# A two-layer block on one core: POOL takes the products of the probabilities with the reciprocal sums, under a new order of the attention stage

## What is computed

```python
q = h @ wq_comp @ wq_up                       # 16 heads of 128
q = rmsnorm(partial_rope(q), q_norm_w)
k = rmsnorm(partial_rope(h @ wk), k_norm_w)   # one key head
v = h @ wv
scores = einsum('bhtd,bsd->bhts', q, k) / sqrt(128)   # masked: 0 <= t - s < 64
probs = softmax(concat([scores, sink]), axis=-1)
attn = einsum('bhts,bsd->bhtd', probs[..., :t], v)
x = x + ga * (attn @ out_w1 @ out_w2)
```

## Time and profile before

| | us |
|---|---|
| three runs | 717.58, 723.96 (median), 724.84 |
| the profiled execution | 719.88 |
| its span, first to last instruction | 718.1 |
| busy: TensorE 563.4, VectorE 444.9, ScalarE 307.5, POOL 260.4 | |

### The profile page before, as it was taken

One profiled execution on the slowest core, in us unless ns is written; L12 is line 12 of the kernel. 1 busy time (PEld: TensorE's weight loads), 2 busy tenths in 40 slices (PEclk: granted clock), 3 DMA queues, 4 the chain that ended last, 5 costly groups with the idle time before them and its releaser, 6 DMA issues.

```text
span 718.1 us, 9581 instructions
## 1 busy us (share of the span) xinstructions
PE 563.4 (78%) x3092; PEld 423.2 (59%) x3092; DVE 444.9 (62%) x981; ACT 307.5 (43%) x951; POOL 260.4 (36%) x305
## 2 busy tenths in 40 slices
PE   2996998596506657476377999999999799998996
PEld 0553676374304434345254777677677688887885
DVE  5729466352398436331688799999786565745444
ACT  2664445242203423232257887887886211111110
POOL 2225507635573311116664554631110355610000
PEclk9899999786557967789687999999999999999999
DMA  8700135331305999882222232330000000000000
GB/s 309 306 1 0 38 128 199 110 104 54 93 0 148 283 310 303 265 306 81 74 58 53 31 50 40 49 41 1 1 1 1 1 0 1 1 8 22 1 1 29
DMA packets 28753, 62.90 MB, mean 88 GB/s; under 512 B 7779, under 2 KB 11025, under 8 KB 28192
## 3 DMA queue, kind: packets, MB, share of 16 engines
q1 hardware_dynamic: 20000, 41.30, 18.3%
q0 software_dynamic: 8704, 21.00, 11.5%
HBM read 48.63 MB, written 17.83 MB: 93 GB/s over the span
## 4 chain that ended last, share of the span: by engine, by line
PE 44%; DVE 24%; issue 10%; DMA 7%; POOL 5%; ACT 4%; another core or an unknown queue 3%; SPq 2%; POOLq 0%; DVEq 0%; ACTq 0%
PE bank L1269 40%; DMA arena<-in_usc 3%; POOL expert_in L392 2%; DVE arena L1099 2%; ACT arena L748 2%; DMA arena<-in_dsc 2%; DVE arena L1195 2%; POOL arena L422 1%; POOL arena L427 1%; SPq L313 1%; DMA arena<-in_wmod 1%; DVE arena L1164 1%; DVE arena L934 1%; DMA expert_out<-arena 1%
## 5 line engine op out<-in xcount | busy, mean ns | idle before, releaser
L1269 PE MATMUL bank<-arena 128*128 128x128 f32 (+9 forms) x1848 | 366.9, 389 | 38.0 <-DMA arena<-in_wmod 8.3
L1269 PEld LDWEIGHTS bank<-arena 128*128 128x128 f32 (+4 forms) x1848 | 249.9, 188 | 122.4 <-issue 76.1
L392 POOL DMA_INDIRECT expert_in<-arena x64 | 65.5, 1024 | 67.3 <-DVE arena L996 46.6
L855 ACT ACTIVATE arena<-bank 128x512 f32<-128x512 f32 x32 | 19.2, 599 | 113.4 <-PE bank L1269 113.4
L1250 DVE TENSOR_TENSOR arena<-arena,bank 128x512 f32<-128x512 f32 x32 | 22.0, 687 | 56.6 <-ACT arena L855 56.6
L1269 PE MATMUL bank<-h_hi,gu_hi 128*128 128x512 f32 x128 | 50.7, 396 | 1.0 <-issue 0.5
L1269 PE MATMUL bank<-h_low,gu_hi 128*128 128x512 f32 x128 | 50.5, 394 | 0.0
L1269 PE MATMUL bank<-h_hi,low 128*128 128x512 f32 x128 | 50.1, 391 | 0.0
L456 POOL TENSOR_TENSOR low<-arena,gu_hi 128x128 fp32r<-128x128 f32 x64 | 29.9, 499 | 55.4 <-DVE dn_hi L1199 55.4
L422 POOL DMA_INDIRECT arena<-expert_out,arena x32 | 37.1, 1160 | 9.2 <-issue 8.4
L1269 PE MATMUL bank<-dn_hi,it_hi 128*128 128x256 f32 x128 | 36.4, 285 | 3.9 <-DVE it_low L1252 3.9
(11 more groups left out here) (235 smaller groups left out, 1040.5 us busy)
## 6 DMA issues: line engine op xcount, KB each, us to landing
arena<-in_wgu SPq DMA_DIRECT2D x32, 384.0 KB, 4.8
arena<-in_wd SPq DMA_DIRECT2D x32, 192.0 KB, 6.7
expert_in<-arena SPq DMA_DIRECT2D x1, 4096.0 KB, 23.8
arena<-expert_in POOLq DMA_DIRECT2D x16, 256.0 KB, 7.1
expert_out<-arena POOLq DMA_DIRECT2D x16, 256.0 KB, 7.1
arena<-in_w SPq DMA_DIRECT2D x1, 2048.0 KB, 9.1
arena<-in_wmod SPq DMA_DIRECT2D x1, 1536.0 KB, 15.3
arena<-in_w_in SPq DMA_DIRECT2D x1, 1288.0 KB, 8.9
```

The costliest lines, as they stand in the source:

```text
L392: pool.indirect_dma_start(xin, bass.IndirectOffsetOnAxis(scatter8[:, t, k:k + 1], 0), h[:, t, :], None, bounds_check=SLOTS - 1, oob_is_err ...
L855: act.activation(gl[n % 3], bank[2 * (n % 3)][:, :], ACT.Gelu_apprx_tanh).then_inc(gl_ready, 1)
L1269: return pe.matmul(o, lhsT, rhs, start=start, stop=stop, **kw)
```

## The change

The 128x1024 product leaves VectorE's two `over_sums` steps, which now end with the reciprocal. POOL gets two steps of the same names that do it, and a new semaphore `pm_ready` tells TensorE's `probs_T_a` and `probs_T_b` that it is done (before: `pn_ready`). VectorE's `maxima_a` and `maxima_b` wait for it too, since they lead to new sums. The orders of the loops on all four engines are new, some steps use other banks, and the waits for free banks follow from that. VectorE's loop and TensorE's have one pass less (T + 7, T + 4); `over_sums_b` now belongs to the same turn as `over_sums_a`. Nothing is computed otherwise than before.

The diff, cut to the steps that the text speaks of:

```diff
             # POOL
+            def over_sums_a(t):
+                pool.wait_ge(pn_ready, 2 * t + 1)
+                pool.tensor_tensor(Pb[0], Pb[0], over(den[0], P), ALU.mult).then_inc(pm_ready, 1)
+
+            def over_sums_b(t):
+                pool.wait_ge(pn_ready, 2 * t + 2)
+                pool.tensor_tensor(Pb[1], Pb[1], over(den[1], P), ALU.mult).then_inc(pm_ready, 1)
+
             for s in range(T + 3):
                 if 0 <= s - 1 < T:
                     gather_rest(s - 1)
-                if 0 <= s - 3:
-                    squares(s - 3)
                 if s < T:
                     gather_first(s)
+                if 0 <= s - 3:
+                    over_sums_a(s - 3)
                 if 0 <= s - 2 < T:
                     rotate(s - 2)
+                if 0 <= s - 2 < T:
+                    squares(s - 2)
+                if 0 <= s - 3:
+                    over_sums_b(s - 3)
...
             # VectorE
             def over_sums_a(t):
                 dve.wait_ge(p_ready, 2 * t + 1)
                 link(dve.tensor_tensor(den[0], den[0], es[0], ALU.add))
-                link(dve.reciprocal(den[0], den[0]))
-                dve.tensor_tensor(Pb[0], Pb[0], over(den[0], P), ALU.mult).then_inc(pn_ready, 1)
+                dve.reciprocal(den[0], den[0]).then_inc(pn_ready, 1)
...
             # TensorE
             def probs_T_b(t):
-                pe.wait_ge(pn_ready, 2 * t + 2)
...
+                pe.wait_ge(pm_ready, 2 * t + 2)
+                pe.wait_ge(PT_ready, 2 * t + 1)
...
             def states_T(t):
                 pe.wait_ge(ha_ready, t + 1)
                 if t >= 1:
-                    pe.wait_ge(q_copied, 4 * t)
+                    pe.wait_ge(qT_ready, 5 * t - 3)
```

More of the change, by code:

```diff
@@ L793, in copy_mlp_rows_T @@
                 act.wait_ge(kv_mm, min(t + 2, T))
-                act.activation(hT[:, :, WIN + t * P:WIN + (t + 1) * P], bank[5][:, 0:DM].rearrange("p (a b) -> p a b", b=P),
+                act.activation(hT[:, :, WIN + t * P:WIN + (t + 1) * P], bank[2][:, 0:DM].rearrange("p (a b) -> p a b", b=P),
                                ACT.Copy).then_inc(h4T_ready, 1)
             for s in range(T + 5):
+                if 0 <= s - 4 < T:
+                    root_4(s - 4)
+                if 0 <= s - 1 < T:
+                    rows_T(s - 1)
+                if 0 <= s - 5 < T - 1:
+                    copy_mlp_rows_T(s - 5)
+                if 0 <= s - 2 < T:
+                    copy_scales(s - 2)
+                if 0 <= s - 3 < T:
+                    copy_attended_b(s - 3)
+                if 0 <= s - 1 < T:
+                    copy_narrow(s - 1)
+                if 0 <= s - 2 < T:
+                    exponents_a(s - 2)
+                if 0 <= s - 1 < T:
+                    copy_queries_1(s - 1)
+                if 0 <= s - 1 < T:
+                    keys(s - 1)
+                if 0 <= s - 1 < T:
+                    copy_queries_2(s - 1)
+                if 0 <= s - 1 < T:
+                    copy_queries_0(s - 1)
+                if 0 <= s - 1 < T:
+                    copy_queries_3(s - 1)
+                if 0 <= s - 2 < T:
+                    exponents_b(s - 2)
                 if s < T:
@@ L800, in _ @@
                 if 0 <= s - 2 < T:
[L801 to L804, removed]
                     copy_probs_T_a(s - 2)
[L806 to L809, removed]
+                if 0 <= s - 1 < T:
+                    values(s - 1)
                 if 0 <= s - 1 < T:
                     squares(s - 1)
-                if s < T:
-                    rows_T(s)
+                if 0 <= s - 1 < T:
+                    copy_queries_T_0(s - 1)
+                if 0 <= s - 1 < T:
+                    copy_queries_T_3(s - 1)
+                if 0 <= s - 1 < T:
+                    copy_queries_T_2(s - 1)
+                if 0 <= s - 1 < T:
+                    copy_queries_T_1(s - 1)
+                if 0 <= s - 1 < T:
+                    copy_keys_T(s - 1)
                 if 0 <= s - 2 < T:
@@ L1234, in _ @@
                 if s < T:
[L1235 removed]
+                    combine_moments(s)
+                if 0 <= s - 2 < T:
+                    over_sums_a(s - 2)
                 if 0 <= s - 2 < T:
                     maxima_b(s - 2)
[L1238 to L1239 removed]
+                if 0 <= s - 7 < 4:
+                    split_rows(s - 7, 1)
                 if 0 <= s - 1 < T:
@@ L1243, in _ @@
                     rotated(s - 1)
+                if 0 <= s - 4 < T - 1:
+                    norm_4(s - 4)
+                if 0 <= s - 2 < T:
+                    over_sums_b(s - 2)
+                if s - 2 == T - 1:
+                    for i in range(3):
+                        weights_high(i)
+                if 0 <= s - 3 < T:
+                    residual(s - 3)
+                if s < T:
+                    norm_a(s)
             norm_4(T - 1)
```

336 lines of the change are left out of this document (147 added, 189 removed).

## The result

The changed kernel takes 757.35 us (median of four runs, 756.12 to 762.05), the kernel before 724.21 beside it: a ratio of 1.0504, 95% interval 1.0446 to 1.0561. It is slower by 5.0%, where 736 us (+1.7%) was forecast, and it lies above the range of 714 to 751. The profiled execution took 756.12 us (span 754.3, against 718.1).

The account below looks back on a forecast made before the run. TensorE's floor is 23.8 us a turn, VectorE bounds late turns. Late turns become 20.0 + 3.05 + 4.85 = 27.9 us; net +12 makes the profiled execution 732, the median 736 us, range 714 to 751.

Parts of the forecast that it names:

- What bounds the kernel: Attention turns before the change: TensorE's floor 23.8 us, VectorE bounding late turns at 25.2, so relieving VectorE brings at most 1.5.
- POOL's product at 2.0 us: Each of two 128x1024 products a turn moved to POOL takes 2.0 us, between bounds of 1.89 and 2.1.
- Holds, 4.85 us in a late turn: VectorE operations standing under POOL products: 1.65 at `maxima_b`, 1.75 at `norm_4`, 1.45 at `residual`; 3.55 in early turns.
- The gap of 5.3 us and the closed loop: `maxima_a` starts 5.3 us after `norm_a`, VectorE standing 3.05; every hold in the loop with TensorE is paid in full.
- done at about 4.2: TensorE's part after `norm_a`, from `states_T` through `scores_a` and the scales, finishes about 4.2 us after `norm_a` ends.
- stay hidden: The next tile's second four gathers, 5.3 us and 1.8 to land, cost nothing, as `combine` comes over 9 us later.
- The drain: From `combine` 7 at 505 to the MLP's start: 78.9 us.
- The MLP is untouched: The MLP after the attention stage was expected to add nothing to the time.
- The filling: The stage's start up to `combine` 2, which was to start at 371 us instead of 365.99.
- TensorE as the bound (716): Rival: holds fall into the gap or under reductions, turns of 23.8 to 24 us, 716 us; chance 0.22.
- half of the holds (724): Rival: only 2.4 of 4.85 us of holds paid, 2 us less in each of six turns, 724 us; chance 0.18.
- The falling clock (753): Rival: TensorE's 4 us idle halves its clock, +2.8 us in six turns, 17 more, 753 us; chance 0.12.

Follow-up runs that it names:

- e9: Kernel before, its order kept, both products on POOL, all gathers ahead of `rotate`, the last four behind `combine`'s moments: 735.55 us, 1.0218.
- e6: e5 with `residual` behind `norm_a`, `root_4` behind `exponents_a`, and `square_sums` between `over_sums_b` and `norm_a`: 741.04 us, 1.0244.
- e12: Changed kernel, the next tile's first four gathers waiting for the copied scales, POOL's `over_sums_b` cut to its first 8 columns: 730.08 us, 1.0158.
- e10: e5 with two unread 128x512 matmuls ahead of `states_T` in TensorE's idle time, from tile 4 on: 738.67 us, 1.0274.
- e5: Changed kernel, but from tile 4 on the next tile's first four gathers wait until the turn's scales are copied: 743.17 us, 1.0286.
- e7: Kernel before, its order kept, both products on POOL, `over_sums_b` ahead of `squares`, `gather_rest` ahead of `over_sums_a`: 733.68 us, 1.0145.
- e8: Changed kernel with all eight gathers of a turn in a row behind the copied scales: 781.5 us in one run.
- e11: Changed kernel with `bounds_check=0` in `gather_first`, so nearly all rows of four gathers are skipped while POOL executes eight: 752.5 us in one run.

## Why the prediction was wrong

- **What bounds the kernel** was read rightly: TensorE close behind VectorE, little to gain, by the earlier trace rows. No run tests it, since none frees VectorE: even e9, without the two products, has VectorE busy 24.5 us of a turn, by the holds.
- **POOL's product at 2.0 us**: 1.89 or 1.90 in 14 of 16, so the row of `squares` was the nearer one, not L376. It isn't fixed, though: in e9 `over_sums_a` takes 2.27 us in seven of eight tiles. The figure of 4497 ns that the prediction takes from the Trainium skill ("GPSIMD Engine Reference", section 3.1) is for an add, not for a product; the 2.25 us worked out from it is above what was measured here.
- **Holds, 4.85 us in a late turn**: measured 0.5 + 1.1 (`maxima_b`), 1.6 (`norm_4`), 1.5 (`residual`) = 4.7. A held operation is released 0.13 us ahead of the product's end (507.04 + 2.00 - 0.42 = 508.62, against 508.75), as in the rows of before. The prediction's reason for leaving reductions out, that a reading of one SBUF operand is not held, was wrong: the L933 of its own is a `tensor_scalar` with one tensor operand and is held, and so is the L1121 of e9 above. That reductions run free, taken without a row, is shown: 1.29 us for the pair at 578.34 and for each turn's, beside POOL's product, as before (1.28), and e6 has the same for reductions of 1024 columns in SBUF. So the Trainium skill's rule that `tensor_reduce` never blocks ("SBUF — State Buffer", section "Who interferes with whom") agrees with the trace.
- **The gap of 5.3 us and the closed loop**: 4.95 where nothing else disturbs it, and e12 shows that a hold ahead of `norm_a` is paid nearly in full (1.4 of 1.5 us). With the row of gathers parted and the idle time filled (e10) the forecast's path comes out nearly to the microsecond, in part by luck, since the two early turns were forecast 1.5 us too short in sum and the three late ones 2.6 too long: `combine` 2 at 372.0 (371), `combine` 7 at 504.9 (505), `norm_a` 7 ends at 525.8 (526), `scores_a` 7 at 553.5 (554).
- **The step that failed** is the sentence on TensorE's part, "done at about 4.2", together with the one that the gathers "stay hidden". I asked of POOL's eight gathers only when their rows land, and not what else they stand beside. In four of five turns they put `rx_mm` off by 3.5 to 4.2 us. By the starts of `combine`, the five turns took 148.9 us; e10 132.9; the forecast 134. So 16.0 us of the 24 missing come from here, the clock's 1.3 us among them, less 1.1 by which the loop was forecast too long. In the kernel before POOL's four and four had `squares` between them, and its turns gave no warning. Its filling did: an increment of the queries comes at 354.01, 1.6 us behind its matmul, at the end of twenty gathers in a row (325.6 to 352.6), which I had not looked for.
- **The drain**: forecast 78.9 us from `combine` 7 to the MLP (583.9 less 505), measured 84.2, and 82.4 in e10: 5.3 missing. The item overlooked is the 3.86 us in the rows above: `maxima_b` 7 behind `over_sums_a` 7. In the turns `combine` covers that wait; in the last tile there is no `combine`. What makes the other 1.4 us was not taken apart.
- **"The MLP is untouched"**: its work is, but it takes 149.1 us in place of 146.2. Its first half, which begins at the 1.2 GHz level, takes 1.6 us longer, and its second 1.3: behind the same 2.77 us of idle time between the halves the granted clock is 0.50 for 3.4 us here and 1.00 in the kernel before.
- The filling was short by 1.0. 1.0 + 16.0 - 1.1 + 5.3 + 2.9 = 24.1 us, the difference of 756.1 and 732.
- **Rivals.** TensorE as the bound (716) and half of the holds (724) did not occur: their condition, holds under reductions or in the gap, was met by none of the four holds. The falling clock (753) had the right sign and the wrong size: the granted clock was 0.50 for some 3.4 us in four of the five turns (from 400.4, 451.6, 461.9 and 492.6), but only that at 451.6 lies right behind `norm_a`, where `probs_T_b` took 1.92 us, and there it costs some 1.3 us (e5), not 2.8; the MLP's start adds 1.6. The time fell near this rival's by another cause.

## What to carry to other kernels

Before work moves onto an engine that also issues transfers, lay out that engine's queue for one turn and see which rows of transfers grow together by it, and what runs beside them; and then count, for each neighbour with SBUF operands on the other engine, the hold that it will bring. A product of 1.2 us on VectorE that becomes one of 1.9 on POOL can be a gain only where it stands beside reductions or idle time, and no version here showed one. Where one operation closes a loop over two engines (`norm_a` last on one, `states_T` first on the other), what is added ahead of it is paid nearly in full (1.4 of 1.5 us in e12), and the last turn must be worked out by itself, as its cover is missing there.

## What the runs showed of the hardware

- TensorE's increments came late, by up to 5.5 us behind the records of their matmuls, from about the fifth POOL gather in an unbroken row on, most often until about the end of the row (8 gathers: five kernels; 6 gathers: 2.2 to 2.5 us in three turns, 0.6 in one), and beside rows of four in few turns, and by at most 1.9 us (e7, e9). Late increments of different semaphores came in steps of 1.4 us or twice that: in the changed kernel at 396.55, 399.43 and 400.87, and at 488.62, 491.50 and 492.95. It followed the row to another place (e8) and stayed when a fifth of the software queue's bytes went, though none of its packets (e11). What it is inside the chip, these traces don't show, and whether TensorE computes late or only reports late neither.
- Behind the same 2.63 us of idle time TensorE was at 1.2 GHz in one turn and at 2.4 in the next two (e5).
